# Order and buffers at the end of a two-pass state-space block's first pass, and its second pass's first loads moved ahead of the barrier

## The chip, the cores and the metric

One NeuronCore of a Trainium2 chip runs the whole kernel. The metric is the device time of one execution in microseconds. Engine names are those of the profile: PE (TensorE), ACT (ScalarE), DVE (VectorE), POOL (GpSimd), SP (SyncE, which here only issues DMAs).

## The reference

The input is 4096 tokens of 1024 values. Three blocks are added onto it; the middle one is the state-space block that the kernel's two passes are built around:

```python
x = x + 0.5 * ffn(layernorm(x))                  # weights rounded to -1, 0, 1
# the middle block, on layernorm(x):
u, z = split(x @ W_in.T)
u = silu(conv_b + causal_conv4(u, conv_w))
x_dbl = u @ W_xproj.T                            # 64 values of dt_r, 16 of B, 16 of C
dt = softplus(dt_r @ W_dt.T + b_dt)
h = exp(dt * A) * h + dt * B * u                 # along the tokens, 16 states a channel
y = sum_n(h_n * C_n) + u * Dskip
x = x + (y * silu(z)) @ W_out.T
x = x + 0.5 * ffn(layernorm(x))
```

## The kernel before

The first pass (`first_pass`) goes over the tokens in 8 chunks of 512 and leaves in DRAM what the second needs. For a chunk it makes the first ffn, the normalised input `xz`, the u half of the input product, the convolution and silu (`u`), and then 18 "units" of that chunk one step later: `x` (the product with W_xproj, copied into `xdbl`), `c` (C turned round), eight `y` (u turned round and multiplied with Dskip) and eight `d` (product with W_dt, then softplus to `dt`; POOL multiplies `dt` with u to `dtu`). All 18 units go through two banks of PSUM, `p_s[0]` and `p_s[1]`, by their number in the list `units`: unit v uses bank v % 2, and PE may write a bank only when the unit two places ahead in the list has been read out (`s_free`), by ACT for `x` and `d`, by DVE for `y` and `c`.

The work of the end is `tail()`, written out for each engine. Chunks are counted from 0; `LAST` is chunk 7. In the tail PE makes the eight u products of chunk 7 (`u_product`, 24 matmuls each), and behind each the units of chunk 6 that `BEATS` names; such a group is a beat here. ACT copies each product out (`u_work`, the tile `up`), makes the softplus of the beat's `d` units and then the silu that follows the beat's convolution. DVE makes the convolution (`conv`, four taps), and the rest of the softplus for the `d` units of the beat before. Behind the eight beats the 18 units of chunk 7 stand alone, with softplus in pairs and rings of four buffers.

A softplus takes ACT three kinds of table: relu and abs are in every one, exp, ln and silu each need their own, and a load (`ACT_TABLE_LOAD`) stands ahead of each change. On DVE it is four instructions, called d here: L633, L635, L638 (waits for ln) and L642 (writes `dt`), all through one buffer `res`.

Each engine takes its instructions in the order in which they are written. The only order across engines is by semaphores. SP's DMAs go out in its own order as well. Behind the first pass all engines meet (the end of `nc.Block()`), after SP has waited for the last stores; only then does the second pass begin. It goes over 16 chunks of 256 tokens, 16 states each: POOL multiplies `dtu` with B (`times_b`, L1182), ACT makes exp(dt*A) (`decays`, L1271), DVE scans (L1399). Its SP prologue loads B's first two states (`bb`), two halves of `dtu` and four pairs of `dt`, then C, an edge column, `y` and `xz`, then two more states of B and the 4 MB weights `wz`.

Of the kernel before, what the change touches and what calls it, by code (L numbers as in the profile page):

```python
# [14 lines left out]
P = 128  # L15
# [8 lines left out]
T2 = 256  # L24
C2 = L // T2
# [49 lines left out]
def first_pass(nc, sem, ins, tern, wu_all, consts, neg_a, ident, split_dram, dram):  # L75
# [10 lines left out]
    with ExitStack() as ctx:  # L86
# [15 lines left out]
        xz = [sb(f"xz{i}", [P, 2, 2, G, T2], F16) for i in range(2)]  # L102
# [68 lines left out]
        a_done = sem("a_done")  # L171

# [48 lines left out]
        BEATS = [(0, 1), (2, 3, 4), (5, 6), (7, 8), (9, 10), (11, 12), (13, 14), (15, 16, 17)]  # L221
        LAST, LPAR = C1 - 1, (C1 - 1) % 2
        last_rel = rel + [xin[0][:, 0:T1], xin[0][:, T1:2 * T1]]
        last_ex = ex + [xin[1][:, 0:T1], xin[1][:, T1:2 * T1]]
        last_lg = lg + [xn[0][:, 0:T1], xn[0][:, T1:2 * T1]]

        def beat_units(b, kinds):

            return [(v, *units[v]) for v in BEATS[b] if units[v][0] in kinds]

        def softplus_ring(d, g):

# [18 lines left out]
        with nc.Block() as block:  # L251
            @block.sync
            def _(sp):
# [45 lines left out]
                def s_store(d, v, kind, g):  # L299
                        if kind == "x":  # L300
                            wait_alone(sp, s_free[v % 2], d * NU + v // 2 + 1)
                            sp.dma_start(dram["b"][bass.ds(d * 2, 2)].rearrange("h n t -> n h t"),
                                         xdbl[R:R + NS, :].rearrange("n (h t) -> n h t", h=2)).then_inc(b_stored, 16)
                        if kind == "c":
                            wait_alone(sp, s_free[v % 2], d * NU + v // 2 + 1)
                            with nc.allow_non_contiguous_dma(reason="64 bytes a token"):
                                sp.dma_start(dram["ct"][bass.ds(d * T1, T1), :].rearrange("(t p) n -> p t n", p=P),
                                             ct[:]).then_inc(ct_stored, 16)
                        if kind == "y" and g % 2:
                            wait_alone(sp, s_free[v % 2], d * NU + v // 2 + 1)  # L310
                            sp.dma_start(dram["y0"][bass.ds(d * T1, T1), (g - 1) * P:(g + 1) * P].rearrange(
                                "(t p) n -> p t n", p=P), y0[g // 2 % 2]).then_inc(y0_stored[g // 2 % 2], 16)
                        if kind == "d":
                            wait_alone(sp, dt_done, d * G + g + 1)
                            wait_alone(sp, dtu_done, d * G + g + 1)
                            for name, tile in (("dt", dt), ("dtu", dtu)):
                                sp.dma_start(dram[name][bass.ds(d * 2, 2), :, g].rearrange("h p t -> p h t"),
                                             tile[g % 2][:].rearrange("p (h t) -> p h t", h=2)
                                             ).then_inc(dt_stored[g % 2], 16)
# [107 lines left out]
            def _(act):  # L427
# [30 lines left out]
                def s_unit(d, v, kind, g):  # L458
                        if kind == "x":
                            wait(act, s_full[v % 2], d * NU + v // 2 + 1)  # L460
# [3 lines left out]
                            nc.scalar.activation(xdbl[:], p_s[v % 2][0:R + 2 * NS, :], ACT.Copy).then_inc(s_free[v % 2], 1)  # L464
# [5 lines left out]
                def relu_abs(d, v, g):  # L470
                    q = d * G + g
                    into, mag, _ = softplus_ring(d, g)
                    wait(act, s_full[v % 2], d * NU + v // 2 + 1)
                    wait(act, dt_done, q - 3 if d == LAST and g >= 4 else q - 1)
# [4 lines left out]
                    if d == LAST and g == 2:  # L479
                        act.wait_ge(xb_done, L // P)  # L480
                        act.wait_ge(stats_ready[0], L // P)
                        act.wait_ge(tr_full[0][1], L // P)
                    nc.scalar.activation(into, p_s[v % 2][:], ACT.Relu, bias=dt_b[:, g:g + 1])
                    nc.scalar.activation(mag, p_s[v % 2][:], ACT.Abs, bias=dt_b[:, g:g + 1]).then_inc(s_free[v % 2], 1)
# [11 lines left out]
                def tail():  # L496
# [9 lines left out]
                    s_unit(LAST, units.index(("x", 0)), "x", 0)  # L506
                    for g in range(0, G, 2):
# [1118 lines left out]
```

## Time and profile before

| | us |
|---|---|
| median of 3 runs (2858.55 to 2863.47) | 2860.9 |
| the profiled execution, its own time | 2861.37 |
| its span in the trace | 2859.4 |

Time outside the span is 1.97 us. The mean granted clock of PE is 0.92 of full speed. Busy shares of the span are PE 84%, DVE 83%, ACT 71%, POOL 65%. Section 2 of the page, with 40 slices of 71.5 us, shows DVE at 5 to 7 tenths in the first sixteen slices and at 9 or more from the seventeenth on, when the second pass has begun; the change lies in between, from 929 us to 1101 us.

### The profile page before, as it was taken

Reading aid. Unit: us, or ns where it says so; the run is one execution under the profiler, and the core shown is the slowest. Engines: PE = TensorE matmul, PEld = TensorE weight load, DVE = VectorE, ACT = ScalarE, POOL = GpSimd, SP = SyncE. Lnnn points to the kernel's source line nnn. Section 1 sums busy time; section 2 is a strip of 40 time slices with the busy share of each in tenths; the row PEclk is TensorE's granted clock in tenths of the full one; section 3 lists DMA queues with packets and bytes.
Section 4 is the critical chain, followed back from the end, with each engine's and each line's share of the span. In section 5 each row is a group of like instructions: output and inputs, shape, how many; then the busy total and the mean of one; then the engine's idle time right before and its main releaser. Section 6 shows DMA issues by size and latency. Waiting matters only on the chain.

```text
span 2859.4 us, 37731 instructions
## 1 busy us (share of the span) xinstructions
PE 2412.9 (84%) x12448; PEld 1388.7 (49%) x12448; DVE 2383.8 (83%) x3197; ACT 2040.1 (71%) x3771; POOL 1845.7 (65%) x1449
## 2 busy tenths in 40 slices
PE   3467899998998854798998998898898898898998
PEld 1233444444444323555555555555555555555554
DVE  6556667667676667999999999999999999999992
ACT  2233667667667666788888888888888888888883
POOL 1112223222222128999999999999999999999991
PEclk9688999999999866799999999999999999999999
DMA  6553323333332237667767767767767667767744
GB/s 202 181 209 133 132 99 126 104 127 117 106 134 76 108 135 257 148 147 178 162 142 177 169 146 176 166 145 182 161 147 181 160 146 178 163 140 173 170 104 100
DMA packets 200289, 429.25 MB, mean 150 GB/s; under 512 B 44512, under 2 KB 93920, under 8 KB 199840
## 3 DMA queue, kind: packets, MB, share of 16 engines
q1 hardware_dynamic: 160928, 284.23, 29.9%
q0 software_dynamic: 39168, 142.62, 26.8%
q8 instruction: 100, 1.64, 0.2%
q14 instruction: 93, 0.76, 0.1%
HBM read 190.86 MB, written 110.10 MB: 105 GB/s over the span
## 4 chain that ended last, share of the span: by engine, by line
DVE 25%; POOL 16%; PE 13%; issue 6%; DMA 1%; ACT 1%; POOLq 0%; SPq 0%; DVEq 0%; ACTq 0%
DVE h L1399 16%; POOL dbu L1182 13%; PE p_g L1537 6%; DVE y L1412 6%; PE p_ht L1503 4%; PE p_g L1546 2%; POOL y L1201 2%; DVE x L1446 1%; POOL y L1216 1%; DVE x L1436 1%; PE p_g L1527 1%; DVE q L1425 1%; DVE small L55 1%; POOL dbu L1187 1%; DMA y<-y_part 0%
## 5 line engine op out<-in xcount | busy, mean ns | idle before, releaser
L1182 POOL TENSOR_TENSOR dbu<-dtu,bb 128x1024 f32<-128x1024 f32 x512 | 1269.2, 2614 | 26.3 <-DVE h L1399 17.6
L1399 DVE TENSOR_TENSOR_SCAN h<-p_da,dbu 128x512 f32<-128x512 f32 x1024 | 1186.6, 1205 | 31.1 <-ACT p_da L1271 17.1
L1271 ACT ACTIVATE p_da<-dt,neg_a 128x255 f32<-128x255 f32 x2048 | 879.6, 467 | 240.6 <-DVE h L1399 235.0
L1503 PE MATMUL p_ht<-ident,h 128*128 128x128 f32 x4096 | 564.8, 297 | 126.1 <-DVE h L1399 125.5
L1503 PEld LDWEIGHTS p_ht<-ident,h 128*128 128x128 f32 x4096 | 514.0, 154 | 203.3 <-DVE h L1399 178.4
L1412 DVE SCALAR_TENSOR_TENSOR y<-p_ht,ct,y 128x1024 f32<-128x1024 f32 x272 | 344.7, 1267 | 18.3 <-PE p_ht L1503 18.2
L813 PE MATMUL p_u<-xz,wu 128*128 128x512 f16 x1536 | 351.7, 387 | 6.8 <-DVE xz L586 6.2
L1537 PE MATMUL p_g<-wo,tokt 128*128 128x512 f16 x1536 | 351.7, 387 | 3.3 <-ACT tokt L1314 2.1
L1546 PE MATMUL p_g<-wz,xz 128*128 128x512 f16 x1536 | 344.5, 381 | 0.0
L70 POOL TENSOR_TENSOR small<-small,consts 128x1 f32<-128x1 f32 x96 | 68.9, 718 | 421.2 <-DVE small L63 421.2
L390 POOL TENSOR_TENSOR late<-dt,u 128x512 f32<-128x512 f32 x64 | 82.6, 1291 | 368.4 <-DVE dt L642 368.4
L804 PE MATMUL p_ffn<-tern,xt 128*128 128x512 f16 x1024 | 256.2, 414 | 23.9 <-DVE xt L586 23.9
L1294 ACT ACTIVATE y_part<-p_ht,ct 128x1024 f32<-128x1024 f32 x224 | 246.6, 1101 | 32.2 <-PE p_ht L1503 28.9
L813 PEld LDWEIGHTS p_u<-xz,wu 128*128 128x128 f16 x1536 | 151.0, 100 | 199.4 <-issue 28.6
L1537 PEld LDWEIGHTS p_g<-wo,tokt 128*128 128x128 f16 x1536 | 153.1, 100 | 181.5 <-issue 17.2
L1201 POOL DMA_DIRECT2D y<-y_part x224 | 202.0, 902 | 58.8 <-issue 44.4
L1527 PE MATMUL p_g<-tern,tokt 128*128 128x512 f16 x1024 | 231.5, 380 | 3.4 <-ACT tokt L1314 2.3
L1546 PEld LDWEIGHTS p_g<-wz,xz 128*128 128x128 f16 x1536 | 151.5, 99 | 168.9 <-issue 3.4
L431 ACT ACTIVATE xn<-xin,small 128x1024 f32<-128x1024 f32 x32 | 39.7, 1242 | 238.7 <-POOL small L72 238.7
L792 PE MATMUL p_tr<-ident,xn 128*128 128x128 f32 x512 | 90.8, 335 | 127.2 <-DVE xt L586 75.9
L804 PEld LDWEIGHTS p_ffn<-tern,xt 128*128 128x128 f16 x1024 | 109.0, 107 | 161.1 <-issue 63.2
L1527 PEld LDWEIGHTS p_g<-tern,tokt 128*128 128x128 f16 x1024 | 99.7, 98 | 113.3 <-issue 3.5
(127 smaller groups left out, 2804.5 us busy)
## 6 DMA issues: line engine op xcount, KB each, us to landing
y<-y_part POOLq DMA_DIRECT2D x224, 512.0 KB, 5.7
bb<-b_scratch SPq DMA_DIRECT2D x128, 256.0 KB, 4.0
xin<-in_x SPq DMA_DIRECT2D x32, 512.0 KB, 5.6
x_scratch<-x SPq DMA_DIRECT2D x32, 512.0 KB, 4.9
xz_scratch<-xz SPq DMA_DIRECT2D x16, 1024.0 KB, 6.2
y_scratch<-late SPq DMA_DIRECT2D x32, 512.0 KB, 5.4
dt_scratch<-dt SPq DMA_DIRECT2D x64, 256.0 KB, 2.1
dtu_scratch<-late SPq DMA_DIRECT2D x64, 256.0 KB, 2.4
```

The costliest lines, as they stand in the source:

```text
L804: mm = nc.tensor.matmul(p_ffn[h][:], xt[:, a, g, :], tern[:, g, h * HALF:(h + 1) * HALF], start=(g == 0 and a == 0), stop=(g == G - 1 and ...
L813: mm = nc.tensor.matmul(p_u[g % 2][:].rearrange("p (h t) -> p h t", h=2), wu[wa][:, kk, g * P:(g + 1) * P], xz[par][:, xa, :, kk, :], star ...
L1182: nc.gpsimd.tensor_tensor(state[:, 4 * f:4 * f + 4, :], dtu[k % 3][:], bb[n // NB % 2][:, n % NB:n % NB + 1, :].to_broadcast([P, G // 2, T2]),
L1201: pool.dma_start(into[:], part[part_of(c, n) % 3][:], accum_op=ALU.add).then_inc(done, 16)
L1271: ins_ = nc.scalar.activation(p_da[p % 2][:, k * T2 + 1:(k + 1) * T2], dt[m % NR][:, k, 1:], ACT.Exp, scale=neg_a[:, g, n:n + 1])
L1294: nc.scalar.activation(into[:], p_ht[1][:], ACT.Copy, scale=ct[par][:, 1, n:n + 1]).then_inc(y_added[1], 1)
L1399: nc.vector.tensor_tensor_scan(h[n % 2][:, 2 * p:2 * p + 2, :].rearrange("p g t -> p (g t)"), p_da[p % 2][:], dbu[n % 2][:, 2 * p:2 * p + ...
L1412: nc.vector.scalar_tensor_tensor(out=y[par][t][:], in0=p_ht[t][:], scalar=ct[par][:, t, n:n + 1], in1=y[par][t][:], op0=ALU.mult, op1=ALU. ...
L1503: mm = nc.tensor.transpose(p_ht[t][:, g * P:(g + 1) * P], h[n % 2][:, g, t * P:(t + 1) * P], ident[:])
L1527: mm = nc.tensor.matmul(p_g[b][:], tokt[:, a, g, :], tern[:, g, cols], start=(n == 0), stop=(n == 2 * G - 1))
L1537: mm = nc.tensor.matmul(p_g[b][:], tokt[:, ta, g, :], wo[:, wa, g, cols], start=(n == 0), stop=(n == 3 * G - 1))
L1546: mm = nc.tensor.matmul(p_g[b][:], xz[:, xa, g, t * P:(t + 1) * P], wz[:, wa, g, cols], start=(n == 0), stop=(n == 3 * G - 1))
```

## The change

It does four things, all at the first pass' end and the second's beginning.

1. PE makes chunk 6's x product ahead of chunk 7's eight u products; it stood behind the first of them.
2. In the beats, ACT takes the softplus of two `d` units together, over two beats, followed by two silus. DVE makes two convolutions ahead of two d's, and its y units stand behind the odd convolutions. Chunk 6's last y unit stands behind chunk 6's last d.
3. Chunk 7's `d` units get banks of their own (the four of the ffn and the transposes) and rings of six buffers, and ACT takes them in groups of three, three and two. Both y units 0 and 1 stand ahead of the x product, and x shares its bank with y unit 0.
4. Chunk 0's `dt`, `dtu` and first B are loaded by SP in the first pass' tail, between chunk 6's stores and chunk 7's, into a tile that is `xz[0]` until then. They are taken out of the second pass' prologue.

```diff
-        last_rel = rel + [xin[0][:, 0:T1], xin[0][:, T1:2 * T1]]
...
+        spare = [t[:, h * T1:(h + 1) * T1] for t in (*xin, *xn, *x1) for h in range(2)]
+        last_rel, last_ex, last_lg = (old + spare[4 * k:4 * k + 4] for k, old in enumerate((rel, ex, lg)))
+        GROUPS = [(0, 1, 2), (3, 4, 5), (6, 7)]
+        p_d = [*p_ffn, *p_tr]
+        on_p_s = [("y", 0), ("y", 1), ("x", 0), ("c", 0)] + [("y", g) for g in range(2, G)]
...
+        def bank_of(d, v, kind, g):
+
+            if d < LAST:
+                return p_s[v % 2], s_full[v % 2], s_free[v % 2], d * NU + v // 2 + 1
+            if kind == "d":
+                return p_d[g % 4], last_full[g % 4], last_free[g % 4], g // 4 + 1
+            v = on_p_s.index((kind, g))
+            return p_s[v % 2], s_full[v % 2], s_free[v % 2], d * NU + v // 2 + 1
...
+                def load_ahead():
+                    wait(sp, u_full, LAST * G)
+                    wait(sp, xz_stored[1 - LPAR], 32 * C1 // 2)
+                    wait(sp, b_stored, 16)
+                    for b in range(2):
+                        wait(sp, dt_stored[b], 32 * G // 2)
+                    ahead["load_b"](sp)
+                    for f in range(2):
+                        ahead["load_dtu"](sp, f)
+                        ahead["load_dt"](sp, 2 * f)
+                        ahead["load_dt"](sp, 2 * f + 1)
...
-                    for b in range(G):
+                    s_unit(LAST - 1, 1, "x", 0)
+                    u_work(LAST, 0)
+                    silu(LAST, LPAR, 0)
+                    for b in (1, 3, 5, 7):
+                        pair = [(units.index(("d", g)), g) for g in (b - 1, b)]
                         u_work(LAST, b)
-                        for unit in beat_units(b, "xd"):
-                            s_unit(LAST - 1, *unit)
-                        silu(LAST, LPAR, b)
...
+                        relu_abs(LAST - 1, *pair[0])
+                        if b < G - 1:
+                            u_work(LAST, b + 1)
+                        relu_abs(LAST - 1, *pair[1])
+                        for v, g in pair:
+                            softplus_exp(LAST - 1, v, g)
+                        for v, g in pair:
+                            softplus_ln(LAST - 1, g)
+                        for k in range(b, min(b + 2, G)):
+                            silu(LAST, LPAR, k)
+                    s_unit(LAST, 0, "x", 0)
+                    for group in GROUPS:
+                        for g in group:
+                            relu_abs(LAST, 0, g)
...
+                    conv(LAST, 0)
+                    for b in (1, 3, 5, 7):
                         conv(LAST, b)
...
+                        for v in {1: (2, 3, 5), 3: (7,), 5: (10, 12), 7: (14,)}[b]:
+                            s_unit(LAST - 1, v, *units[v])
+                        if b < G - 1:
+                            conv(LAST, b + 1)
+                        for g in (b - 1, b):
+                            s_unit(LAST - 1, units.index(("d", g)), "d", g)
+                    s_unit(LAST - 1, 17, "y", 7)
...
                 def prologue():
-                    load_b(0, 0)
-                    for f in range(2):
-                        load_dtu(0, f)
-                        load_dt(0, 2 * f)
-                        load_dt(0, 2 * f + 1)
                     load_scan(0, 0)
```

The first place is DVE in the middle of the beats: `late<-p_s0` is a y unit, `acc` with `up` is a convolution, `res` and `dt` are a d. Before, y unit 4 (the only `late` row here) stood behind d 2 and ahead of convolution 5:

```order
L633 TENSOR_SCALAR res<-late 128x512 [waits exp_done,dt_done]
L635 TENSOR_TENSOR res<-late,res 128x512 [waits softplus_chain]
L638 TENSOR_TENSOR res<-late2,res 128x512 [waits softplus_chain,ln_done]
L642 TENSOR_TENSOR dt0<-res,late 128x512 [waits dt_stored0,dtu_done,softplus_chain]
L625 TENSOR_TENSOR late<-p_s0,dskip 128x4x128 [waits y0_stored0,s_full0]
L593 COPY up1<-halo 128x3
L597 TENSOR_SCALAR acc1<-up1,conv_w,conv_b 128x512 [waits silu_done,up_done,conv_chain]
L601 SCALAR_TENSOR_TENSOR acc1<-up1,conv_w,acc1 128x512 [waits conv_chain] x2
```

Now, in the changed program (line numbers are its own), d 3 is followed by convolution 5, and y units 4 and 5 come behind it:

```order
L683 TENSOR_TENSOR dt1<-res,late 128x512 [waits dt_stored1,dtu_done,softplus_chain]
L633 COPY up1<-halo 128x3
L637 TENSOR_SCALAR acc1<-up1,conv_w,conv_b 128x512 [waits silu_done,up_done,conv_chain]
L641 SCALAR_TENSOR_TENSOR acc1<-up1,conv_w,acc1 128x512 [waits conv_chain] x2
L643 COPY halo<-up1 128x3
L645 SCALAR_TENSOR_TENSOR acc1<-up1,conv_w,acc1 128x512 [waits conv_chain]
L666 TENSOR_TENSOR late<-p_s0,dskip 128x4x128 [waits y0_stored0,s_full0] x2
L633 COPY up0<-halo 128x3
```

PE's own order of these units has not changed: y unit 4 and y unit 5 both go to `p_s0`, one behind the other there.

The second place is PE between the last u product and chunk 7's x product. `u0` is chunk 6's u and `u1` chunk 7's; `xdbl,wdt` is a d unit, `ident,u` a y unit, `wx` the x product. Before:

```order
L813 MATMUL p_u1<-xz1,wu 128x512 x23
L844 MATMUL p_s1<-xdbl,wdt 128x512 [waits s_free1]
L844 MATMUL p_s0<-xdbl,wdt 128x512 [waits s_free1,s_free0]
L836 MATMUL p_s1<-ident,u0 128x128 [waits silu_done,s_free1]
L836 MATMUL p_s1<-ident,u0 128x128 x3
L836 MATMUL p_s0<-ident,u1 128x128 [waits silu_done,s_free0]
L836 MATMUL p_s0<-ident,u1 128x128 x3
L831 MATMUL p_s1<-u1,wx 96x512 [waits silu_done,s_free1]
```

Now:

```order
L879 MATMUL p_s1<-ident,u0 128x128 x3
L879 MATMUL p_s0<-ident,u1 128x128 [waits silu_done,s_free0,x1_done]
L879 MATMUL p_s0<-ident,u1 128x128 x3
L879 MATMUL p_s1<-ident,u1 128x128 [waits silu_done,s_free1]
L879 MATMUL p_s1<-ident,u1 128x128 x3
L874 MATMUL p_s0<-u1,wx 96x512 [waits silu_done,s_free0]
L874 MATMUL p_s0<-u1,wx 96x512 [waits silu_done] x7
L884 MATMUL p_s1<-ident,xdbl 128x96 [waits s_free0,s_free1]
L889 MATMUL p_ffn0<-xdbl,wdt 128x512 [waits s_free0]
L889 MATMUL p_ffn1<-xdbl,wdt 128x512 [waits s_free0]
```

The x product now stands behind y units 0 and 1 of chunk 7 and needs DVE to have read unit 0 out of `p_s0`; y unit 1 needs `p_s1`, in which chunk 6's y unit 7 was. DVE reads that unit, in the changed program, behind chunk 6's last d; before it did so ahead of chunk 6's last two. 

The third place is SP where chunk 7's stores begin. The first row is chunk 6's last store:

```order
L322 DMA y0_scratch<-late 128x4x256 [waits s_free1]
L1650 DMA bb0<-b_scratch 128x512 [waits dt_stored0,b_stored,dt_stored1,xz_stored0,u_full]
L1655 DMA shared<-dtu_scratch 128x1024
L1659 DMA shared<-dt_scratch 128x512 x2
L1655 DMA shared<-dtu_scratch 128x1024
L1659 DMA shared<-dt_scratch 128x512 x2
L322 DMA y0_scratch<-late 128x4x256 [waits s_free1]
```

Seven loads, 2.25 MB, stand ahead of chunk 7's stores, and the second pass' prologue on SP begins with C.

## Rows read from the trace of the kernel before

**Rows 1.** The chain that ended last, 1072 to 1102 us: start, us, what.

```profile
1085.25 4.58 DVE h L1399 x4
...
1090.13 11.21 DMA bb<-b_scratch
```

**Rows 2.** Timeline of ACT, one beat: start, us, instruction, [idle before, releaser].

```profile
983.17 0.68 ACT L442 ACTIVATE up<-p_u,consts 128x512 f32<-128x512 f32 x1
983.75 0.68 ACT L483 ACTIVATE late<-p_s,dt_b 128x512 f32<-128x512 f32 x1
985.02 1.28 ACT L489 ACT_TABLE_LOAD   x1
986.32 0.63 ACT L489 ACTIVATE late<-late 128x512 f32<-128x512 f32 x1
...
991.13 0.69 ACT L442 ACTIVATE up<-p_u,consts 128x512 f32<-128x512 f32 x1 [0.30 <-PE p_u L813]
```

**Rows 3.** Timeline of PE in the tail.

```profile
935.15 7.46 PE L813 MATMUL p_u<-xz,wu 128*128 128x512 f16 x24 [6.17 <-DVE xz L586]
942.45 7.03 PE L831 MATMUL p_s<-u,wx 128*96 128x512 f32 x16
949.31 5.34 PE L813 MATMUL p_u<-xz,wu 128*128 128x512 f16 x24
959.04 1.20 PE L844 MATMUL p_s<-xdbl,wdt 64*128 64x512 f32 x2 [3.61 <-DVE late L625]
992.57 5.34 PE L813 MATMUL p_u<-xz,wu 128*128 128x512 f16 x24
999.39 5.34 PE L813 MATMUL p_u<-xz,wu 128*128 128x512 f16 x24
1015.32 8.36 PE L831 MATMUL p_s<-u,wx 128*96 128x512 f32 x16
```

**Rows 4.** Timeline of ACT: chunk 6's and chunk 7's last silu, chunk 7's first relu.

```profile
938.19 0.63 ACT L452 ACTIVATE u<-acc 128x512 f32<-128x512 f32 x1 [3.18 <-DVE acc L605]
...
1019.55 0.63 ACT L452 ACTIVATE u<-acc 128x512 f32<-128x512 f32 x1
...
1026.06 0.69 ACT L483 ACTIVATE late<-p_s,dt_b 128x512 f32<-128x512 f32 x1 [1.75 <-PE p_s L844]
```

**Rows 5.** Timeline of DVE: one convolution's end, then chunk 7's last y and d's.

```profile
994.07 0.75 DVE L605 SCALAR_TENSOR_TENSOR acc<-up,conv_w,acc 128x512 f32<-128x512 f32 x1
...
1060.11 0.68 DVE L625 TENSOR_TENSOR late<-p_s,dskip 128x512 f32<-128x512 f32 x1
...
1063.37 0.69 DVE L642 TENSOR_TENSOR dt<-res,xin 128x512 f32<-128x512 f32 x1
...
1064.56 1.63 DVE L635 TENSOR_TENSOR res<-xin,res 128x512 f32<-128x512 f32 x1
1066.30 0.69 DVE L638 TENSOR_TENSOR res<-xn,res 128x512 f32<-128x512 f32 x1
1067.02 0.69 DVE L642 TENSOR_TENSOR dt<-res,xin 128x512 f32<-128x512 f32 x1
```

**Rows 6.** POOL beside the last of these d's, and its second state after the barrier.

```profile
1064.14 1.50 POOL L390 TENSOR_TENSOR late<-dt,u 128x512 f32<-128x512 f32 x1 [2.61 <-DVE dt L642]
...
1085.17 4.64 POOL L1182 TENSOR_TENSOR dbu<-dtu,bb 128x1024 f32<-128x1024 f32 x2
```

**Rows 7.** SP after the barrier: its first DMA, C's, and the second of B.

```profile
1072.64 0.34 SPq L1075 DMA_DIRECT2D bb<-b_scratch  x1
...
1077.09 0.77 SPq L1045 DMA_DIRECT2D ct<-ct_scratch  x1
...
1082.67 0.53 SPq L1075 DMA_DIRECT2D bb<-b_scratch  x1
```

**Rows 8.** Two windows: us, PE, PEld, DVE, ACT, POOL busy, clock, DMA share, GB/s.

```profile
1000.00:1050.00 50.00, 32.91 (x89) 13.90 (x88) 33.69 (x51) 36.44 (x47) 9.58 (x7) 0.68 0.36 126
...
1072.00:1102.00 30.00, 6.72 (x32) 6.01 (x32) 16.80 (x20) 13.33 (x29) 20.67 (x15) 0.59 0.86 307
```

More of the change, by code:

```diff
@@ L24 @@
 T2 = 256
+NB = 2
+NR = 6
 C2 = L // T2
@@ L101, in first_pass @@
         xt = sb("xt", [P, 2, G, P], F16)
-        xz = [sb(f"xz{i}", [P, 2, 2, G, T2], F16) for i in range(2)]
+        xz_shared = ahead["tile"][:].bitcast(F16).rearrange("p (a h k t) -> p a h k t", a=2, h=2, k=G)
+        xz = [xz_shared, sb("xz1", [P, 2, 2, G, T2], F16)]
         up = [sb(f"up{i}", [P, T1 + 3]) for i in range(2)]
@@ L309, in s_store @@
[L309 to L319, printed above, removed]
+                    _, _, free, count = bank_of(d, v, kind, g)
@@ L459, in s_unit @@
                         if kind == "x":
-                            wait(act, s_full[v % 2], d * NU + v // 2 + 1)
+                            bank, full, free, count = bank_of(d, v, kind, g)
+                            wait(act, full, count)
                             wait(act, b_stored, d * 16)
@@ L463, in s_unit @@
                             wait(act, s_full[b], m)
-                            nc.scalar.activation(xdbl[:], p_s[v % 2][0:R + 2 * NS, :], ACT.Copy).then_inc(s_free[v % 2], 1)
+                            nc.scalar.activation(xdbl[:], bank[0:R + 2 * NS, :], ACT.Copy).then_inc(free, 1)
                         if kind == "d":
@@ L472, in relu_abs @@
                     into, mag, _ = softplus_ring(d, g)
-                    wait(act, s_full[v % 2], d * NU + v // 2 + 1)
-                    wait(act, dt_done, q - 3 if d == LAST and g >= 4 else q - 1)
+                    bank, full, free, count = bank_of(d, v, "d", g)
+                    wait(act, full, count)
+                    wait(act, dt_done, q - 1 if d < LAST or g < 2 else q - 5)
                     if d == 0:
@@ L480, in relu_abs @@
                         act.wait_ge(xb_done, L // P)
[L481 to L484, printed above, removed]
+                        for n in range(2):
+                            act.wait_ge(stats_ready[n], L // P)
+                            act.wait_ge(tr_full[n][1], L // P)
+                            act.wait_ge(x1_stored[n], 16 * (L // P) // 2)
+                    nc.scalar.activation(into, bank[:], ACT.Relu, bias=dt_b[:, g:g + 1])
+                    nc.scalar.activation(mag, bank[:], ACT.Abs, bias=dt_b[:, g:g + 1]).then_inc(free, 1)
                 def softplus_exp(d, v, g):
                     mag = softplus_ring(d, g)[1]
-                    wait(act, s_free[v % 2], d * NU + v // 2 + 1)
+                    _, _, free, count = bank_of(d, v, "d", g)
+                    wait(act, free, count)
                     nc.scalar.activation(mag, mag, ACT.Exp, scale=-1.0).then_inc(exp_done, 1)
@@ L823, in s_unit @@
                 def s_unit(d, dpar, v, kind, g):
-                        wait(pe, s_free[v % 2], d * NU + v // 2)
-                        ps = p_s[v % 2]
+                        ps, full, free, count = bank_of(d, v, kind, g)
+                        wait(pe, free, count - 1)
                         if kind == "x":
@@ L943, in second_pass @@
         edge_loaded, edge_arg, edge_done = sem("edge_loaded"), sem("edge_arg"), sem("edge_done")
-        dt_loaded = [sem(f"dt2_pair_loaded{k}") for k in range(NR)]
-        dtu_loaded = [sem(f"dtu2_half_loaded{k}") for k in range(3)]
+        dt_loaded, dtu_loaded, b_loaded = ahead["dt_loaded"], ahead["dtu_loaded"], ahead["b_loaded"]
         ct_loaded = [sem(f"ct2_loaded{i}") for i in range(2)]
@@ L948, in second_pass @@
         y_loaded = [sem(f"y2_loaded{i}") for i in range(2)]
-        b_loaded = [sem(f"b2_loaded{i}") for i in range(2)]
         xz_loaded = sem("xz2_loaded")
```

146 lines of the change are left out of this document (83 added, 63 removed).

## The prediction

> **What bounds it now.** The change touches 929 to 1101 us, so I read that stretch in four views. The chain of waits comes first: it enters the second pass by its first scans and then a load of B that takes 11.21 us [rows 1]. The reader should see that this pass starts with transfers: SP issues the first at 1072.64 [rows 7], and DVE's first scan begins at 1085.25 [rows 1], 12.6 us later.
>
> The timelines of ACT, PE and DVE show the tail. A beat takes ACT 7.66 us (991.13 less 0.30 idle less 983.17) [rows 2], and PE 6.82 (999.39 less 992.57) [rows 3]: ACT sets the beats. Chunk 7's x product runs from 1015.32 to 1023.68 [rows 3]. From there to the last `dt`, at 1067.71 [rows 5], it is 44.0 us of ACT and DVE taking turns, with PE at a mean granted clock of 0.68 [rows 8]. Everything behind the last `dt` (a product on POOL, two stores, the barrier) is as it was. So the change is worth what it moves that last `dt`, plus what it takes out between barrier and first scan, if the second pass passes it on. DVE and POOL are both at 9 tenths there, so I let it pass in full.
>
> **Durations for the walk.** ACT: relu and abs of a d 1.27 (985.02 less 983.75), a table load to its function's start 1.30, exp or ln 0.63, `up` 0.6 [rows 2]. So from a pair's second abs to the silu is 1.30 + 1.26 + 1.30 + 1.26 + 1.30 = 6.4, and to the end of its first ln 4.5. DVE: convolution 3.0 from the end of `up` (991.82 [rows 2] to 994.82 [rows 5]); from ln to `dt` 1.4 (1066.30 to 1067.71); a d that directly follows another 3.65 (1064.06 to 1067.71), because L635 stretches to 1.63 while POOL multiplies at 1064.14 [rows 5, 6]; a y between costs little (1060.11 to 1064.06 is 3.95 for both) [rows 5]. PE: u product 5.34, a d 1.2, a y 0.6 at the high clock; double at the low one of its two levels.
>
> **Part 1, the x product ahead.** It can run behind chunk 6's first y unit, but its last step needs chunk 6's last silu, at 938.82 [rows 4]; it ends at 939.8. The u products then start there instead of at 935.15, without the 7.03 us between the first two [rows 3]. The second ends at 950.5 instead of 954.65: 4.1 us early. The wait of 3.61 us ahead of the first d (a y on DVE behind the convolution) stays and moves along. With no other block up to the fifth product this ends at 977, still 4 early.
>
> **Part 2, the pairs.** Their ACT work is 2 x (0.6 + 1.27) + 6.4 + 1.2 = 11.3 us for two beats, below PE's 13.6, so ACT would no longer bound. But the order on DVE brings new waits. d 3's bank is freed by y unit 3, which stands behind convolution 3, which stands behind d 0 and d 1: first ln at 970.6, `dt` 972.0, next 975.65, convolution 978.65, y 979.3. PE waits 2.3 us there; the sixth product starts at 981.3 (before 984.26): 3 early. Next, y unit 5 must wait for y unit 4 on the same bank, and that now stands behind convolution 5. relu and abs of d 3 end at 982.0, ln of d 2 at 986.5, `dt` 2 at 987.9, `dt` 3 at 991.5, convolution 5 at 994.5, y unit 4 at 995.1. PE is ready at 988.9, so this is a stall of 6.2 us, and the seventh product starts at 995.9 (before 992.57 [rows 3]). With a low clock behind such a stall (the product from 935.15 took 7.46, not 5.34 [rows 3]) it ends at 1002.4, and the last ends at 1009.3, against 1004.73 before: 4.6 late.
>
> The same loop once more: ln of d 4 at 1009.5, `dt` 4 and 5 at 1011 and 1014.6, convolution 7 at 1017.6, y unit 6 at 1018.2, then d 7 on PE to 1020.3, its abs at 1021.7, silu 7 at 1028.7 (before 1020.18 [rows 4]).
>
> **Part 3, chunk 7's x product.** Before, it started at 1015.32, beside the last softplus. Now it stands behind y unit 1, whose bank waits for chunk 6's last y on DVE, behind d 6 and d 7: ln 1026.2, `dt` 1027.6, `dt` 1031.2, y 1031.8; y unit 1 ends at 1033.0 at the low clock. With the same 8.36 us x ends at 1041.3 against 1023.68: **17.6 us late**.
>
> **Part 4, threes on four banks.** Counted from x's end: first relu +2.4 (1026.06 [rows 4]), three relu and abs 3.6, table, three exp, table, first ln 5.1, `dt` 0 1.4: +12.5. Then DVE is never let go: `dt` 1 and 2 at 3.65, `dt` 3 with two y's 4.1 (the second y hides the rest of POOL's product), four more at 3.65: 26.0. The last `dt` is at +38.5, before +44.0: **5.5 us gained**. DVE's y unit 5 stands ahead of d 0; behind the first relu's d PE has five more and four y's to do, and a d with a y is 6.82 - 5.34 = 1.5 [rows 3]: 7 us, so they end at +9.4, well inside the 12.5. With the low clock from a few us on, as before, they end some 5 later, at +14.5; behind them DVE's y and a whole d (3.2) would put `dt` 0 at +17.7, 5 late: the bound from above.
>
> Tail: 17.6 - 5.5 = 12.1 late. If all PE work ran at the high clock it would be 10.2.
>
> **Part 5, the loads ahead.** After the barrier POOL can start at once, as it did its memset. Two products and the carry's column take what they take for the second state, 4.64 + 0.2 [rows 6], so the first scan comes 5.3 us after the barrier instead of 12.6: **7.3 us gained**. ACT's table and four exps fit into that. SP's second load of B is issued 10.03 us after its first now [rows 7]; the seven issues taken out end at 1077.09 [rows 7], so it goes out 4.45 earlier, at +5.6. The third state needs it at +10.4, so it has 4.8 us. The next load of B, the one of 11.21 us behind `wz` [rows 1], has 2.25 MB less ahead of it, 7.7 us at this stretch's 307 GB/s [rows 8]; it moves with the rest. Bounds: 4.4 if the start can only move as far as SP's issues do, 7.7 if all DMA ahead was the limit.
>
> On the skill: the Trainium skill, "ScalarE: Activation LUTs", section "What ACT_TABLE_LOAD costs", gives 1.28 us for a load and 1.38 more of drain, 2.66 in all. The trace disagrees: exp starts 1.30 after its load does [rows 2]. By the page 14 loads fewer would be worth 37 us of ACT instead of 18; neither is on the path by this walk, where PE and DVE wait for bank order.
>
> **Sum.** 12.1 - 7.3 = +4.8, by the high clock +2.9; I take +4.1. The profiled execution took 2861.4, 0.5 over the median: 2865.5.
>
> **Rivals.** A change of 0.2% (5.7 us) is what can be told from none.
> - *Faster.* The beats run at PE's pace, since y unit 4 is read early or ACT's saving reaches the path. Then the last product ends near 997 (the third starts at 956.1, five beats of 6.82, a product, a cold start), d 7's abs at 1000.7, and x 19.6 us behind that as in my walk, at 1020.3: 3.4 early. With 5.5 and 7.3 the time is 2845. It turns on y unit 4: free before 989 it costs nothing. Against it stands the order on DVE. Chance 0.12.
> - *Slower, in chunk 7's units.* PE is at the low clock there, as it was before (mean 0.68 [rows 8]), and `dt` 0 is 5 us late: 2870.5. For it: low clocks behind each stall; against it: PE's work there is dense now. Or the first y store, behind 2.25 MB, holds y unit 4 of chunk 7; it has about 3 us of room. A DMA behind `wz` took 11.21 us [rows 1]. Chance 0.14.
>   The Trainium skill, "DMA: Bandwidth & Descriptors", section "Queues, rings and completion order", says that an engine consumes descriptors in ring order; by that, the store can't pass those loads.
> - *The loads ahead do little.* The second or third load of B becomes the wait, and 4 of the 7.3 us are lost again: 2869.5. Chance 0.14.
> - *As forecast*, 2862 to 2868.5: 0.60, of which 0.10 lies above 2866.6.
>
> **Chances and range.** Faster 0.12, same 0.50, slower 0.10 + 0.14 + 0.14 = 0.38. The range leaves out the faster case and the end of the slow ones: 2859 to 2870.5.
>
> **What would show it.** PE: y unit 5's transposes with some 6 us of idle released by DVE's y. DVE: chunk 6's last y behind its last d, and x starting about 1033. Seven d's about 3.65 apart at the end; the last `dt` near 1080. From the barrier to the first scan 5.3 us. The forecast is wrong if PE shows no such idle, or if after the barrier POOL waits for `bb` by more than 3 us.

## The result, and the profile after

| | us |
|---|---|
| before, median of 5 runs (2857.60 to 2863.47) | 2859.16 |
| after, median of 5 runs (2864.34 to 2875.13) | 2869.41 |
| after by before | 1.0036, 95% interval 1.0019 to 1.0053 |
| the profiled execution of after: own time, span | 2868.85, 2867.0 |

Slower by 0.36%. It lies inside the range, 3.9 us above the forecast of 2865.5, and beyond the 0.2% (5.7 us) within which I had called a change none, the case that I held likeliest; the interval begins at 0.19%. Profile against profile the difference is 7.5 us, less than the medians' 10.25. The runs of before that went with the experiments (medians 2861.3 to 2862.5, 11 to 24 runs each) lie 2.2 to 3.4 us above the five of this comparison. The kernel e13 below, whose first scan comes within 0.2 us of after's, took 1.0028 of before (1.0018 to 1.0039), 7.8 us. I take 7.5 to 8 as the size.

All positions from here on are counted from PE's last turn of chunk 7's input (`p_tr<-ident,xn`, at 925.34 in before and 926.50 in after), since that turn comes at 920.48 us in the earliest of the profiled kernels (e12) and at 931.34 in the latest (e11).

| from the last turn | before | after | moved |
|---|---|---|---|
| chunk 7's x product ends | 98.3 | 118.6 | +20.2 |
| last `dt` | 142.4 | 156.9 | +14.55 |
| barrier (POOL's memset) | 147.3 | 161.9 | +14.6 |
| first scan | 159.9 | 167.2 | +7.3 |

The rest of the 7.5 us is the later turn (+1.16) and a second pass shorter by 0.8 from its first scan on (1773.3 for 1774.1).

PE in the tail of after, from its timeline (start, us, instruction, [idle before, releaser]); it answers to [rows 3]:

```profile
926.50 1.04 PE L835 MATMUL p_tr<-ident,xn 128*128 128x128 f32 x8
931.79 9.57 PE L874 MATMUL p_s<-u,wx 128*96 128x512 f32 x16 [1.58 <-DVE late L666]
941.20 10.52 PE L856 MATMUL p_u<-xz,wu 128*128 128x512 f16 x48
956.10 1.12 PE L889 MATMUL p_s<-xdbl,wdt 64*128 64x512 f32 x2 [3.61 <-DVE late L666]
...
981.15 2.07 PE L889 MATMUL p_s<-xdbl,wdt 64*128 64x512 f32 x2 [3.40 <-DVE late L666]
...
998.69 1.11 PE L879 MATMUL p_s<-ident,u 128*128 128x128 f32 x4 [6.29 <-DVE late L666]
999.59 6.36 PE L856 MATMUL p_u<-xz,wu 128*128 128x512 f16 x24
1007.43 5.34 PE L856 MATMUL p_u<-xz,wu 128*128 128x512 f16 x24
1022.47 2.07 PE L889 MATMUL p_s<-xdbl,wdt 64*128 64x512 f32 x2 [8.64 <-DVE late L666]
1036.01 1.12 PE L879 MATMUL p_s<-ident,u 128*128 128x128 f32 x4 [8.98 <-DVE late L666]
1036.91 8.16 PE L874 MATMUL p_s<-u,wx 128*96 128x512 f32 x16
```

The reader should see a PE that goes ahead early (two u products in one row, the x product before them) and then stands behind `late`, DVE's y units: 3.61, 3.40, 6.29, 8.64, 8.98 us. From the last turn to chunk 7's x product these waits are 32.5 us in all, with the 1.58 of the second row. In before they were 5.6 us in the same stretch (3.61, 0.32, 1.34, 0.30), and its waits for ACT were 8.0; two of its rows:

```profile
982.52 1.12 PE L844 MATMUL p_s<-xdbl,wdt 64*128 64x512 f32 x2 [1.34 <-DVE late L625]
...
1014.41 1.11 PE L836 MATMUL p_s<-ident,u 128*128 128x128 f32 x4 [4.67 <-ACT late L484]
```

From 3.61 on, what waits in after is a small product of 1 or 2 us, for a bank that DVE frees late, and the u product or x product behind it waits with it.

DVE of after, around y unit 4 and at chunk 6's end, and POOL beside it:

```profile
993.36 0.69 DVE L683 TENSOR_TENSOR dt<-res,late 128x512 f32<-128x512 f32 x1
993.96 0.16 DVE L633 COPY up<-halo 128x3 f32<-128x3 f32 x1
994.16 1.51 DVE L637 TENSOR_SCALAR acc<-up,conv_w,conv_b 128x512 f32<-128x512 f32 x1
...
997.95 0.68 DVE L666 TENSOR_TENSOR late<-p_s,dskip 128x512 f32<-128x512 f32 x1
...
1034.66 0.69 DVE L683 TENSOR_TENSOR dt<-res,late 128x512 f32<-128x512 f32 x1
1035.27 1.28 DVE L666 TENSOR_TENSOR late<-p_s,dskip 128x512 f32<-128x512 f32 x2
```

```profile
994.12 1.26 POOL L415 TENSOR_TENSOR late<-dt,u 128x512 f32<-128x512 f32 x1 [2.15 <-DVE dt L683]
```

y unit 4 ends at 998.6, and PE goes on at 998.69. Ahead of it stand d 2, d 3 and the whole convolution 5, whose first operation took 1.51 us beside POOL's product; elsewhere it takes 0.55.

The end and the head of after, DVE and then POOL, answering to [rows 1, 5, 6]:

```profile
1052.29 0.69 DVE L666 TENSOR_TENSOR late<-p_s,dskip 128x512 f32<-128x512 f32 x1 [0.19 <-DMA y_scratch<-late]
1056.92 0.69 DVE L683 TENSOR_TENSOR dt<-res,late 128x512 f32<-128x512 f32 x1
1060.58 0.69 DVE L683 TENSOR_TENSOR dt<-res,late 128x512 f32<-128x512 f32 x1
...
1082.73 0.69 DVE L683 TENSOR_TENSOR dt<-res,late 128x512 f32<-128x512 f32 x1
1093.68 4.57 DVE L1437 TENSOR_TENSOR_SCAN h<-p_da,dbu 128x512 f32<-128x512 f32 x4 [4.82 <-POOL dbu L1225]
1098.57 2.34 DVE L1437 TENSOR_TENSOR_SCAN h<-p_da,dbu 128x512 f32<-128x512 f32 x2 [0.32 <-POOL dbu L1225]
```

```profile
1088.38 0.20 POOL L1208 MEMSET carry<- 128x128 f32 x1 [3.62 <-POOLq L261]
1088.66 4.70 POOL L1220 TENSOR_TENSOR dbu<-shared,bb 128x1024 f32<-128x1024 f32 x2
...
1099.05 4.67 POOL L1220 TENSOR_TENSOR dbu<-shared,bb 128x1024 f32<-128x1024 f32 x2 [0.52 <-DMA bb<-b_scratch]
```

The first `dt` is done 12.5 us behind the x product's end, the last 38.35 behind it (before: 44.0), and from the barrier to the first scan it is 5.30 us (before: 12.62).

SP of after, where the loads stand ahead of chunk 7's stores:

```profile
1038.38 0.43 SPq L1650 DMA_DIRECT2D bb<-b_scratch  x1
...
1042.47 2.12 SPq L1659 DMA_DIRECT2D shared<-dt_scratch  x2
1044.63 0.71 SPq L322 DMA_DIRECT2D y_scratch<-late  x1
```

Seven issues take 6.2 us, and the first y store of chunk 7, whose data was ready at 1037.85 (DVE's read of y unit 1 runs from 1037.16 for 0.69 us), goes out at 1044.63. It was held, but only 0.19 us of it reached DVE (the row at 1052.29).

### The profile page after: what moved, and what is told of

It is laid out like the page before. It is cut to its first block, busy times and chain, and to the rows that moved or that the text cites. A ratio compares the mean times of both kernels' runs of the same rounds, so it can differ in the third digit from the quotient of the medians.

```text
span 2867.0 us, 37718 instructions
## 1 busy us (share of the span) xinstructions
PE 2412.4 (84%) x12448; PEld 1391.0 (49%) x12448; DVE 2388.5 (83%) x3197; ACT 2022.4 (71%) x3758; POOL 1847.5 (64%) x1449
## 4 chain that ended last, share of the span: by engine, by line
POOL 31%; DVE 14%; PE 10%; issue 7%; ACT 1%; POOLq 0%; DVEq 0%; ACTq 0%
POOL dbu L1220 23%; DVE h L1437 9%; PE p_g L1575 4%; POOL y L1239 3%; DVE y L1450 3%; PE p_ht L1541 3%; PE p_g L1584 2%; POOL y L1254 1%; POOL dbu L1225 1%; PE p_g L1565 1%; POOL x L1258 1%; DVE x L1484 0%; POOL carry L1231 0%; DVE x L1474 0%; POOL small L72 0%
## 5 line engine op out<-in xcount | busy, mean ns | idle before, releaser
L1220 POOL TENSOR_TENSOR dbu<-shared,bb 128x1024 f32<-128x1024 f32 x352 | 894.3, 2618 | 11.1 <-DVE h L1437 10.3
L1309 ACT ACTIVATE p_da<-shared,neg_a 128x255 f32<-128x255 f32 x1408 | 604.9, 467 | 167.2 <-DVE h L1437 162.8
L1220 POOL TENSOR_TENSOR dbu<-dtu,bb 128x1024 f32<-128x1024 f32 x160 | 418.7, 2617 | 5.3 <-DVE h L1437 5.2
L1309 ACT ACTIVATE p_da<-dt,neg_a 128x255 f32<-128x255 f32 x640 | 274.6, 467 | 72.1 <-DVE h L1437 70.8
L856 PE MATMUL p_u<-xz,wu 128*128 128x512 f16 x768 | 175.6, 386 | 0.0
```

The source lines that it names most:

```text
L856: mm = nc.tensor.matmul(p_u[g % 2][:].rearrange("p (h t) -> p h t", h=2), wu[wa][:, kk, g * P:(g + 1) * P], xz[par][:, xa, :, kk, :], star ...
L1220: nc.gpsimd.tensor_tensor(state[:, 4 * f:4 * f + 4, :], dtu[k % 3], bb[n // NB % 2][:, n % NB:n % NB + 1, :].to_broadcast([P, G // 2, T2]) ...
L1309: ins_ = nc.scalar.activation(p_da[p % 2][:, k * T2 + 1:(k + 1) * T2], dt[m % NR][:, k, 1:], ACT.Exp, scale=neg_a[:, g, n:n + 1])
```

## The experiments

My theory: the tail is late because DVE's y units stand behind whole convolutions and pairs of d's, with their banks. The other parts are worth what the walk says. Rivals: the x product's or the threes' place does it; ACT's or DVE's pace does it whatever the order; the loads ahead disturb the tail.

Measured, all of them (positions from the last turn; the time by before's runs taken beside it):

| kernel | x ends | last `dt` | first scan | median us | by before, 95% interval |
|---|---|---|---|---|---|
| e1 ahead only | 97.6 | 141.5 | 151.7 | 2855.33 | 0.9976 (0.9963 to 0.9990) |
| e2 no ahead | 120.3 | 158.6 | 176.3 | 2878.57 | 1.0057 (1.0040 to 1.0074) |
| e3 y early | 99.8 | 138.1 | 148.4 | 2849.85 | 0.9964 (0.9951 to 0.9977) |
| e4 and x first | 93.0 | 138.2 | 148.4 | 2850.75 | 0.9961 (0.9946 to 0.9976) |
| e5 y4, y6 early | 104.6 | 143.0 | 153.2 | 2854.18 | 0.9973 (0.9961 to 0.9984) |
| e7 one a beat | 100.7 | 139.7 | 149.95 | 2850.39 | 0.9958 (0.9944 to 0.9971) |
| e8 and x behind | 104.1 | 142.4 | 152.65 | 2853.87 | 0.9973 (0.9961 to 0.9984) |
| e9 e4, loads first | 93.1 | 131.4 | 141.7 | 2846.07 | 0.9940 (0.9927 to 0.9953) |
| e10 e7, both edits | 94.4 | 132.7 | 143.0 | 2844.62 | 0.9931 (0.9913 to 0.9948) |
| e11 odd dtu short | 117.6 | 155.95 | 166.2 | 2872.44 | 1.0031 (1.0019 to 1.0043) |
| e12 all dtu short | 111.9 | 150.3 | 160.5 | 2865.53 | 1.0006 (0.9994 to 1.0019) |
| e13 x first in after | 118.4 | 156.7 | 167.0 | 2869.18 | 1.0028 (1.0018 to 1.0039) |

Each row is one trace, and the last `dt` of one tail is not fixed to the microsecond: e2 has after's tail but for SP's loads, and its last `dt` is 1.7 us later. So positions that differ by less than 2 us are not told apart by this table.

**e1, the loads ahead alone in before.**

```diff
                         s_store(LAST - 1, v, kind, g)
+                    load_ahead()
...
                 def prologue():
-                    load_b(0, 0)
-                    for f in range(2): ...
```

> The kernel before with part 4 of the change alone: chunk 0's dt, dtu and B loaded in the tail, ahead of chunk 7's stores. Theory 1 (the head gains 7.3 us and the tail's loss is all from the order of units over banks): barrier to first scan 5.3 us instead of 12.6, last dt within 1 us of where it was, time 7 us shorter (2852). Rival (the 2.25 MB in the tail hold up chunk 7's first y stores and with them DVE): last dt 3 us or more later, time only 0 to 4 us shorter.

**e2, after without them.** The reverse edit.

> The changed kernel with its loads put back behind the barrier; tail as changed. Theory 1: the tail is as late as in the changed kernel (last dt some 14.6 us later than before, counted from the tail's start), barrier to first scan 12.6 us again, time 14 to 15 us over before (2874). Rival (loads in the tail cause part of the lateness): last dt is earlier than in the changed kernel by 2 us or more, and the time below 2871.

The first scans of e1 and of e2:

```profile
1075.09 4.57 DVE L1406 TENSOR_TENSOR_SCAN h<-p_da,dbu 128x512 f32<-128x512 f32 x4 [4.82 <-POOL dbu L1194]
```

```profile
1101.26 4.57 DVE L1429 TENSOR_TENSOR_SCAN h<-p_da,dbu 128x512 f32<-128x512 f32 x4 [12.32 <-POOL dbu L1217]
```

From the barrier it is 5.31 us with the loads ahead and 12.81 without, in either tail, so this part is worth 7.3 to 7.5 us and stands by itself. The last `dt` of e1 did not get later (141.5 against before's 142.4). That of e2 did not get earlier than after's, so the loads do not cause the late tail. In the medians e1 is 6.4 us under before (7 expected) and e2 16.9 over (14 to 15 expected).

**e3, y units early**, **e4, and chunk 7's x ahead of its y unit 1**, on the other bank. The order on DVE of e3, `v` a convolution, and the edit of e4:

```diff
-v1 y1 c y2 v2 d0 d1 v3 y3 v4 d2 d3 v5 y4 y5 v6 d4 d5 v7 y6 d6 d7 y7
+v1 y1 c y2 v2 d0 d1 y3 v3 v4 y4 d2 d3 v5 y5 v6 y6 d4 d5 v7 y7 d6 d7
```

```diff
-        on_p_s = [("y", 0), ("y", 1), ("x", 0), ("c", 0)] + ...
+        on_p_s = [("y", 0), ("x", 0), ("y", 1), ("c", 0)] + ...
```

> The changed kernel with DVE's order of chunk 6's y units alone changed: y 3 ahead of convolution 3, y 4 ahead of d 2, y 6 ahead of d 4, y 7 ahead of d 6. Theory 1: the stalls of 3.4, 6.3 and 8.6 us on PE go, the last silu comes some 16 us earlier, the last dt 17 us earlier than in the changed kernel, 6 below before; time about 2848. Rival (the pairs themselves are too slow, ACT's block of 6.4 us between product and silu sets the beats): stalls on PE turn into waits for ACT's up, and the gain against the changed kernel is under 6 us.

> As the one before, and chunk 7's x product stands ahead of y unit 1, on the other bank, as in the kernel before. Theory 1: x then starts beside chunk 6's last two d's, some 6 to 8 us earlier; the last dt 3 to 5 us earlier than with the y units alone (DVE has to finish d 6 and d 7 of chunk 6 either way); time about 2844. Rival: DVE is the bound by then and the x product's place is worth under 1 us.

e3 alone takes 18.8 us off the tail and turns 0.36% slower into 0.36% faster. PE of e3, where after had 3.40, 6.29, 8.64 and 8.98:

```profile
993.00 1.11 PE L875 MATMUL p_s<-ident,u 128*128 128x128 f32 x4 [2.88 <-DVE late L666]
...
1007.44 1.11 PE L875 MATMUL p_s<-ident,u 128*128 128x128 f32 x4 [2.56 <-DVE late L666]
1014.32 9.77 PE L870 MATMUL p_s<-u,wx 128*96 128x512 f32 x16 [5.77 <-DVE late L666]
```

e4 missed. Its x product ends 6.8 us earlier than e3's, and its last `dt` no earlier. DVE of e4, in chunk 7:

```profile
1020.29 0.69 DVE L666 TENSOR_TENSOR late<-p_s,dskip 128x512 f32<-128x512 f32 x1 [0.95 <-PE p_s L875]
1029.48 1.29 DVE L666 TENSOR_TENSOR late<-p_s,dskip 128x512 f32<-128x512 f32 x2 [8.49 <-DMA y_scratch<-late]
```

y unit 4 waits 8.49 us for a store, that of y units 0 and 1, issued on SP at 1019.78 right behind the loads. Over this kernel's y stores between 1005 and 1060 us the trace gives, from issue to landing:

```profile
DMA to landing us min/median/max: 2.8/3.7/9.6
```

The store at 1019.78 is the one of 9.6 us. With the wait only just open in after (0.19 us), the edit fell into the very rival that I had priced for the first y store.

**e9, e4 with the loads at the tail's start.**

```diff
                     store_xz(LAST, LPAR)
+                    load_ahead()
                     for v, (kind, g) in enumerate(units):
                         s_store(LAST - 1, v, kind, g)
-                    load_ahead()
```

> The run with y units early and chunk 7's x ahead of its second y unit, and the six loads ahead moved on SyncE from behind chunk 6's last store to the tail's start, before any of its stores. There VectorE waited 8.5 us for the y store that lay behind these loads, and the first scan came at 148.4 us, as without x ahead. My theory: that wait was the whole of it, and the 4.3 us of the x product ahead now show: 144 us. Rival: VectorE and GpSimd set the pace of chunk 7 and the wait lay in their shadow: 148 again, with the idle time elsewhere.

The wait is gone, as these rows of DVE of e9 show, and the last `dt` comes 6.8 us earlier, all that x had gained:

```profile
1020.62 1.29 DVE L666 TENSOR_TENSOR late<-p_s,dskip 128x512 f32<-128x512 f32 x2 [0.95 <-PE p_s L875]
1023.55 0.69 DVE L666 TENSOR_TENSOR late<-p_s,dskip 128x512 f32<-128x512 f32 x1 [1.64 <-PE p_s L875]
```

I had expected 4.3. The loads, issued from 933.31 on, 80 us sooner than in e4, had all landed by 948.8, and SP's next y store went out at 950.77: nothing waited for them there. (There are seven of them; the expectation says six.)

The Trainium skill, "DMA: Bandwidth & Descriptors", section "Queues, rings and completion order", says that each DMA engine consumes descriptors in ring order, though a later one may finish its write before an earlier one. The trace of e4 agrees with the first half: the seven loads landed from 1018.77 to 1028.06, in the order of their issue, and the store behind them at 1029.38. My "can't pass" among the rivals said more than the page does; in after and e4 no such passing is seen.

**e5, y4 and y6 alone early**, y3 and y7 as in after.

```diff
-v1 y1 c y2 v2 d0 d1 v3 y3 v4 d2 d3 v5 y4 y5 v6 d4 d5 v7 y6 d6 d7 y7
+v1 y1 c y2 v2 d0 d1 v3 y3 v4 y4 d2 d3 v5 y5 v6 y6 d4 d5 v7 d6 d7 y7
```

> After, with two of VectorE's y units alone moved: y4 ahead of conv3's partner pair (d2, d3) and y6 ahead of d4, d5; y3 stays behind conv3 and y7 last. Measured from the last turn's TensorE rows to the first scan, before took 159.9 us, after 167.2, the run with all y units early 148.4. My theory (TensorE's 6.3 and 8.6 us waits are for the banks that y4 and y6 free late): 13 to 14 us less than after, so about 153.5, and a median some 13 us under after's. Rival: the price lies in y3 and y7 (banks held by the units left late here): at most 5 us less than after, 162 or more.

The last `dt` comes 14.0 us earlier, and the first scan is at 153.2, as expected (153.5). So of the 18.8 us of e3, 14.0 are y4's and y6's, and the last 4.8 come when y3 and y7 move too. What y7 costs is still seen in PE of e5:

```profile
1017.08 1.11 PE L875 MATMUL p_s<-ident,u 128*128 128x128 f32 x4 [8.98 <-DVE late L666]
```

**e7, one softplus a beat again, e8, and the x product behind the first u product.** ACT and DVE take chunk 6's beats as before; in e8 so does PE.

```diff
-                    for b in (1, 3, 5, 7):
-                        pair = [(units.index(("d", g)), g) for g in (b - 1, b)]
+                    for b in range(G):
                         u_work(LAST, b)
+                        for unit in beat_units(b, "d"):
+                            s_unit(LAST - 1, *unit)
+                        silu(LAST, LPAR, b)
```

> After, with the kernel before's one softplus a beat for chunk 6 put back; x product ahead, threes on four banks in chunk 7 and the early loads kept. My theory: what the pairs cost goes and the other terms stay (x ahead 4.1, threes 5.5, head 7.3), so from the last turn to the first scan 159.9 - 4.1 - 5.5 - 7.3 = 143.0 us, a time near 2845. Rival A: ScalarE's beats bound chunk 6 whatever TensorE does, so the x product ahead gives nothing: 147, equal to its twin with the x product behind. Rival B: the threes or the x product made the tail late, not the pairs: 160 or more.

> As the run with one softplus a beat, and the x product back behind the first u product; what is left of the change is the threes on four banks and the loads ahead. Loads ahead alone gave 151.7 us from the last turn to the first scan. My theory: the threes take 5.5 off, 146.2. Rival: chunk 7's softplus was not bound by ScalarE's table swaps but by VectorE's 3.65 us a unit, and the threes give 0 to 2 us: 150 or more.

Both expectations for the totals missed, e7 by 7 us and e8 by 6.5, and the reason is in PE of e7:

```profile
1019.37 8.97 PE L868 MATMUL p_s<-u,wx 128*96 128x512 f32 x16 [4.79 <-DVE late L661]
```

Chunk 7's x shares its bank with y unit 0, which DVE reads only behind chunk 6's last d. So between e1 and e8 the x product ends 6.5 us later (e10, with x ahead of y unit 1, ends it 6.4 us earlier than e7), while from there to the last `dt` it is 38.3 us and no longer 43.9. The 5.6 us of the threes (with their banks and rings; no run parts these) are real and are given back by x's place. The x product ahead of the u products (e8 to e7) is worth 2.7 us at the last `dt`, not 4.1. From e7 to after, the pairs, with their order on DVE, cost 17.2 us.

**e10, e7 with e4's and e9's edits.**

> One softplus a beat in chunk 6, the x product ahead, chunk 7's x ahead of its second y unit, the loads ahead at the tail's start, threes on four banks. Against the run with pairs, y units early and the loads at the tail's start (141.7 us from the last turn to the first scan) it tells what pairs are worth once no y unit is late. With one a beat chunk 7's x started 91.8 after the turn, 4.8 of it a wait for the first y unit's bank, which x ahead of the second y unit removes. My theory: ScalarE's beats with two table loads a softplus bind, x starts at 87 and the scan comes at 145, so pairs are worth 3 us there. Rival: with single softplus units the end of chunk 6 is no later, 141 to 142, and pairs give nothing.

x starts at 85.9 and ends at 94.4, and the last `dt` is at 132.7, 1.3 us behind e9's. That is between my 3 us and the rival's nothing, and less than two traces of one tail can differ by; the medians of e9 and e10 can't be told apart either. So what pairs are worth with no y unit late is not shown to be more than nothing. The best two kernels are, by their ratios, 17 to 20 us faster than before. Neither needs the pairs as the change has them.

**e11 and e12, POOL's dt·u of chunk 6 cut to 8 columns**, for blocks 1, 3, 5 or for all. The products of the other columns are left out.

```diff
-                            times_u(d, d % 2, g)
+                            times_u(d, d % 2, g, 8 if d == LAST - 1 and g in (1, 3, 5) else None)
```

> After, with GpSimd's product dt*u of chunk 6 cut to 8 columns for blocks 1, 3 and 5 (the rest of those three products is left out). In after these three ran from 976.6, 994.1 and 1017.9, beside the first operation of a convolution, which took 1.51 us there and 0.55 elsewhere. My theory: VectorE's operation is held by GpSimd's, all three go back to 0.55, and as each lies ahead of a y unit for whose bank TensorE waits, the last dt comes 2.5 to 2.9 us earlier from the last turn (154.0 to 154.4 in place of 156.9; my forecast's walk gave 154.5). Rival: the 1.51 us come from elsewhere (the copy just ahead, reads of the same tile), or lie off the chain: 156.5 or more.

> As the run with blocks 1, 3 and 5 short, now all eight dt*u products of chunk 6 cut to 8 columns (the rest of them is left out). In after the second softplus of a pair has one operation of 1.65 us in place of 0.69, beside the first one's product. My theory: each pair gives back 0.96 more, and three or four pairs lie ahead of y4, y6 and the last units: the last dt at 150 to 152 from the turn. Rival: only the convolution's share lies on the chain: 154.

DVE and POOL of e11, where after has 1.51 and 1.26:

```profile
996.42 0.69 DVE L684 TENSOR_TENSOR dt<-res,late 128x512 f32<-128x512 f32 x1
997.03 0.16 DVE L634 COPY up<-halo 128x3 f32<-128x3 f32 x1
997.23 0.55 DVE L638 TENSOR_SCALAR acc<-up,conv_w,conv_b 128x512 f32<-128x512 f32 x1
```

```profile
997.19 0.21 POOL L416 TENSOR_TENSOR late<-dt,u 128x8 f32<-128x8 f32 x1 [2.15 <-DVE dt L684]
```

The mechanism holds: with POOL's product short, all three operations are back at 0.55. The size did not come through whole (2.5 to 2.9 us expected). x starts 2.2 us earlier (108.2 for 110.4), but its product then took longer, and the last `dt` is only 1.0 us earlier:

```profile
1039.54 9.41 PE L875 MATMUL p_s<-u,wx 128*96 128x512 f32 x16
```

That is 9.41 us against after's 8.16, and the 1.0 us is itself within what two traces can differ by. In e12 x starts 6.8 us earlier and the last `dt` comes at 150.3, as expected, and the time is 1.0006 of before. So in after POOL's products hold DVE back by 6.7 us on the path, about as much as the change loses in all. It is the sum of seven holds of 0.96 us: three convolutions (1.51 for 0.55) and one operation in each of the four pairs (1.65 for 0.69). DVE waits nowhere for POOL's result in this stretch of after, so it is the overlap that costs.

The Trainium skill, "SBUF — State Buffer", section "Who interferes with whom", says that a VectorE operation with two SBUF inputs contends with a GpSimd one that reads SBUF, and that a VectorE operation in a two-port mode, which a tensor_scalar can enter, contends too, one of the two blocking the other. The trace agrees for the one with two inputs, 1.65 for 0.69; for the TENSOR_SCALAR it shows 1.51 for 0.55, and no run shows its mode. The second of the two y units at 1035.27, which reads PSUM and one tensor of SBUF, took its usual 0.6 us with POOL's product from 1035.43 beside it.

**e13, e4's and e9's edits in after.**

> After, with chunk 7's x product ahead of its second y unit and the loads ahead at the tail's start, nothing else. With y units early this pair of edits brought the first scan from 148.4 to 141.7 us after the last turn. My theory: in after the x product waits for what VectorE does last for chunk 6 (d7, then y7 and chunk 7's first y, 0.6 us apart), so whichever bank it takes, it starts 0.9 us earlier at most: last dt at 156 from the turn (after: 156.9), a median within 3 us of after's. Rival: the place behind the second y unit costs after what it costs the kernel with one softplus a beat, 4.8 us: last dt at 152.

The last `dt` is at 156.7, 0.2 us earlier. This was the theory; the rival's 152 did not come. x's place, worth 6.8 us with y early, is worth nothing here, where y unit 1 waits for a bank that y7 frees behind d 7. PE of e13 waits as long as after did:

```profile
1038.62 6.59 PE L874 MATMUL p_s<-u,wx 128*96 128x512 f32 x11 [8.97 <-DVE late L666]
```

## Why the prediction was right and where it fell short

Times of after in this section have the 1.16 us of its later turn taken off.

- **Part 1.** Right on its own ground: the second u product ends at 950.56 (forecast 950.5) and the 3.61 us wait stays. (The table loads that went are 13, 162 to 149 in the traces, and not the 14 that I had weighed: 17 us of ACT for 18.) The x product ahead is worth 2.7 us at the last `dt` in a tail without pairs; in after nothing is left of it behind the waits.
- **Part 2, the pairs.** The mechanism was right in each place, and the signs named for it came (PE idle 6.29 us ahead of y unit 5, chunk 6's last y behind its last d). The waits for d 3, y unit 5 and d 7's bank came behind y 3, y 4 and y 6, and e5 shows that y 4 and y 6 carry 14.0 us. The sizes were short. The wait for d 3's bank was 3.40 for 2.3, the seventh u product started at 998.4 for 995.9, and the last ended at 1011.6 for 1009.3. The term mis-sized is "convolution 3.0" directly behind a pair: it takes 4.0 there, as its first operation runs beside POOL's product. My [rows 5] showed a convolution with no POOL work beside it, and I had used POOL's hold on DVE only inside a d (the 3.65). e11 shows the hold, and 2.2 us of it at x's start. Step by step, y units 3, 4 and 6 end 0.6, 2.4 and 3.1 us behind the walk; three holds of 0.96 are 2.9, and what else slipped (d 3 took 2.07 us on PE, as at the low clock, where I had counted 1.2) is under 1 us and partly made good.
- **Part 3.** x ended at 1043.9 for 1041.3: 20.2 us late, not 17.6. These 2.6 us are part 2's, handed on. e7 and e8 show a second cause that the walk held in the pairs' shadow: by standing behind y units 0 and 1, x loses 6.5 us even with no pairs; e13 shows that in after it costs 0.2, no more than chance.
- **Part 4.** 38.35 for 38.5, 5.7 us gained for 5.5. `dt` 0 was at +12.5 as forecast, so the bound from above (5 us late) did not come.
- **Part 5.** 7.3 us gained as forecast, and e1 and e2 show it alone. One number in it was wrong with no consequence: B's third state was to have 4.8 us of room, and POOL waited 0.52 us for it. Its load went out 3.2 us behind the barrier, sooner than figured, but took 7.4 us to land; I had given it no time to land.
- **Sum.** +4.8 in the walk; I took +4.1 in the direction of the high clock, which did not come (from 1037 to 1085 us the mean granted clock was 0.68 in after, the same as in the stretch of [rows 8]). With the 2.45 us of tail that were missing it is +7.3, and +7.5 was measured on the profiles; that these are so close owes something to luck, as the later turn (+1.16) and the shorter second pass (-0.8), which the walk did not hold, all but cancel. The missing 2.45 us also moved the outcome over the line of 5.7 us: my chance of 0.50 for no change rested on +4.1.
- **Rivals.** *Faster* turned on y unit 4 being free before 989. It was at 998.6 (997.5 by before's turn), and e3 and e5, in which it is early, are faster than before: the fork was the right one. *The first y store* was close: the 3 us of room were gone to 0.19 us, and in e4 it held 8.5 us. *The loads ahead do little* fell. *Slower, in chunk 7's units* gave nearly the measured time (2870.5), but its mechanism did not come. So the range held the result through an upper end that I had set for other reasons.

What stays open: why medians of one kernel differ by 2 to 3 us from one set of runs to the next, and why the second pass behind the first scan took between 1770.4 and 1777.9 us in the profiled runs, with code that is nearly the same.

## What to carry to other kernels

Before units are batched to save table loads, follow for each one whose buffer it holds: a cheap unit (0.68 us of VectorE here) put behind a convolution or a batch cost TensorE 3 to 9 us each time, and moving two of them gave 14 us back. Change one order at a time, since a gain (x first, 6.8 us) can read as 0 while a later wait, a store behind 2.25 MB of loads or a bank read out last, covers it. Loads that are moved ahead should go where nothing on the path follows them on their queue, not just as late as they may.

## What the runs showed of the hardware

VectorE's TENSOR_SCALAR on 128x512 f32 took 1.51 us beside a GpSimd TENSOR_TENSOR and 0.55 beside an 8-column one (e11), though it has one tensor input only; its TENSOR_TENSOR with two SBUF inputs took 1.65 for 0.69. In a tail this held the path by 6.7 us (e12).

The same 16 matmuls of x took 8.16 us in after and 9.82 in e9. Windows over them give the granted clock of PE, in the column behind POOL's. First after, then e9:

```profile
1037.00:1045.00 8.00, 8.00 (x17) 2.72 (x15) 0.69 (x1) 0.00 (x0) 0.00 (x0) 0.86 0.72 206
```

```profile
1005.00:1014.00 9.00, 9.00 (x16) 3.15 (x15) 5.91 (x8) 3.02 (x4) 2.77 (x2) 0.72 0.28 99
```

Between its two levels (1.2 and 2.4 GHz) PE was at the high one for more of the product in after than in e9. Between these two runs the clock took back 1.7 us of what the earlier start won; e11 (9.41 us at 0.76) lost 1.2 of its 2.2 that way. Idle time just ahead does not tell which it will be: PE had stood 8.98 us in after and 8.97 in e11. What sets it is not shown here.
